# A sandwich of attention and feed-forward layers: the window mask moves from TensorE to VectorE's maximum, a state factor to ScalarE, and quantisation work to other turns

## Time and profile before

| | us |
|---|---|
| median of 3 runs (lowest to highest) | 1960.5 (1960.32 to 1961.45) |
| the profiled execution: its own time | 1959.31 |
| its span | 1957.5 |
| TensorE busy (matmuls) | 1876.3 |
| VectorE busy | 1433.4 |
| ScalarE busy | 1229.4 |
| GpSimd busy | 1235.9 |

### The profile page before, as it was taken

The page is one execution under the profiler, slowest core; times in us unless marked ns, Lnnn a source line. Parts: engine busy times, 40 slices in busy tenths (PEclk is TensorE's granted clock), DMA queues, the critical chain, the costliest instruction groups (busy, mean ns, idle before and its releaser), DMA issues.

```text
span 1957.5 us, 42161 instructions
## 1 busy us (share of the span) xinstructions
PE 1876.3 (96%) x11698; PEld 1252.8 (64%) x11698; DVE 1433.4 (73%) x3926; ACT 1229.4 (63%) x4840; POOL 1235.9 (63%) x1150
## 2 busy tenths in 40 slices
PE   4999999999999999999999999999989979999997
PEld 3667677777777777776777676777666635444443
DVE  6998888888888888888888888888899644302022
ACT  5777777777777777777777777776666535312121
POOL 3777777777777777777777777777677521212121
PEclk8999999999999999999999999999999989999999
DMA  5000000000000000000000000000100042000000
GB/s 199 25 26 25 26 25 24 24 24 24 32 25 24 24 24 24 29 24 24 24 24 24 30 29 24 24 24 13 54 13 7 7 134 79 26 1 22 0 21 21
DMA packets 44353, 61.43 MB, mean 31 GB/s; under 512 B 4928, under 2 KB 18496, under 8 KB 44288
## 3 DMA queue, kind: packets, MB, share of 16 engines
q1 hardware_dynamic: 44288, 60.64, 9.6%
HBM read 47.97 MB, written 12.65 MB: 31 GB/s over the span
## 4 chain that ended last, share of the span: by engine, by line
PE 62%; DVE 16%; issue 14%; POOL 3%; ACT 2%; DVEq 1%; DMA 0%; SPq 0%; POOLq 0%; ACTq 0%
PE bank L1250 18%; PE bank L1239 8%; PE bank L1278 6%; PE bank L1221 4%; PE bank L1294 4%; PE bank L1315 4%; PE bank L1379 3%; PE bank L1287 3%; DVE f_s L963 2%; PE bank L1205 2%; PE bank L1304 2%; POOL hl L527 2%; DVE f_nrm L953 2%; PE bank L1270 1%; PE bank L1297 1%
## 5 line engine op out<-in xcount | busy, mean ns | idle before, releaser
L488 POOL TENSOR_TENSOR f_acc<-f_acc,f_s 128x512 f32<-128x512 f32 (+1 forms) x416 | 534.3, 1284 | 30.6 <-POOL f_acc L488 0.4
L1250 PE MATMUL bank<-wh,xh 128*128 (+2 forms) x1024 | 334.9, 327 | 7.3 <-DVE cumh L1099 6.2
L1250 PE MATMUL bank<-wl,xh 128*128 (+2 forms) x1024 | 335.0, 327 | 0.0
L1250 PE MATMUL bank<-wh,xl 128*128 (+2 forms) x1024 | 334.7, 327 | 0.0
L469 POOL TENSOR_TENSOR pr<-pr,rp 128x512 f32<-128x512 f32 x128 | 133.0, 1039 | 229.5 <-DVE rp L894 229.5
L963 DVE TENSOR_SCALAR f_s<-f_nrm 128x512 f32<-128x512 f32 (+1 forms) x480 | 240.9, 561 | 3.7
L575 ACT ACTIVATE qe<-bank,nqm 128x128 f32<-128x128 f32 x512 | 180.8, 365 | 80.3 <-DVE qs L823 57.2
L527 POOL TENSOR_TENSOR hl<-hf,hh 128x512 f16<-128x512 f32 (+1 forms) x44 | 50.8, 1155 | 283.7 <-ACT hh L754 283.7
L1379 PE MATMUL bank<-xh,w 128*128 (+3 forms) x704 | 224.8, 382 | 3.8 <-ACT sg L748 3.8
L603 ACT ACTIVATE pr<-bank,pmx 128x128 f32<-128x128 f32 x512 | 180.9, 367 | 37.5 <-DVE pmx L887 29.6
L1239 PE MATMUL bank<-wh,oT 128*128 (+1 forms) x512 | 194.0, 379 | 3.8 <-DVE xl L1019 1.4
(11 more groups left out here) (177 smaller groups left out, 4973.7 us busy)
## 6 DMA issues: line engine op xcount, KB each, us to landing
f_raw<-wf SPq DMA_DIRECT2D x30, 256.0 KB, 2.6
dequantised<-f_dq SPq DMA_DIRECT2D x30, 256.0 KB, 2.0
wt<-dequantised SPq DMA_DIRECT2D x30, 256.0 KB, 3.0
raw_qkv<-wq SPq DMA_DIRECT2D x29, 256.0 KB, 2.5
raw_o<-wo SPq DMA_DIRECT2D x29, 256.0 KB, 2.6
rows<-x SPq DMA_DIRECT2D x4, 1024.0 KB, 9.3
xr<-x SPq DMA_DIRECT2D x16, 256.0 KB, 3.6
out<-yo SPq DMA_DIRECT2D x16, 256.0 KB, 2.1
```

Of the source, the lines that this page charges most:

```text
L488: nc.gpsimd.tensor_tensor(f_acc[:, 0:w], f_acc[:, 0:w], f_s[:, k % 8, 0:w], ALU.add)\
L1250: last = nc.tensor.matmul(dst, av, w[:, sl + c, lo:hi], start=(n == 0), stop=(n == 3 * NC - 1))
```

## The change

The mask is no longer added by a matmul. `p_max` first writes one element (`pause`) and then runs four `tensor_tensor_reduce`, one per head and 128 columns: each adds the mask to the scores, negates the sum, writes it back to SC, and gives its minimum to `pmx`. `p_exps` reads the negated scores with scale -1. For the first tile of a step, where the mask differs by sequence, ScalarE copies the first 128 columns of it to `win0` (`head_mask`), and TensorE's `scores` waits for that copy. `em` is made by ScalarE as an exponential with a bias of 0 or -1e30, right after the other decays, and VectorE's multiply and its wait go. `nf4_blocks` of piece i + 1 is made at p = 1 of step i, behind the compares (piece 0 still at p = 0), and the compares are spread 2, 3, 5, 5.

```diff
-NF4_STEPS = (range(0, 2), range(2, 6), range(6, 11), range(11, 15))
+NF4_STEPS = (range(0, 2), range(2, 5), range(5, 10), range(10, 15))
...
+            def head_mask(t):
+
+                if t.p == 0:
+                    nc.scalar.activation(win0[:], win[:, t.i % 2, 0:P], ACT.Copy).then_inc(s["head_mask"], 1)
+
...
                 nc.scalar.activation(edT[:, r, :], SM[:, P:P + 130], ACT.Exp)
+                if t.p == 0 and not (isinstance(t.i, int) and t.i == 0):
+                    nc.scalar.activation(em[:, 0, :], SM[:, 2 * P:2 * P + 1], ACT.Exp,
+                                         bias=keep[:].unsqueeze(2)[:, t.i % 2, :])
                 nc.scalar.activation(ked, ked, ACT.Exp, scale=-1.0).then_inc(s["dec_ev"], 1)
...
-                                                bias=pmx[:, r, j:j + 1],
+                                                bias=pmx[:, r, j:j + 1], scale=-1.0,
...
                 k_exps(t)
+                head_mask(t)
...
-                nc.vector.tensor_reduce(pmx[:, r, :], SC[:].rearrange("p (h n) -> p h n", h=GRP), AX.X, ALU.max,
-                                        negate=True).then_inc(s["pmx_d"], 1)
+                nc.vector.memset(pause[:], 0.0)
+                for j in range(GRP):
+                    sl = slice(j * P, (j + 1) * P)
+                    mask = win[:, 1, sl] if t.p or j >= 2 else win0[:]
+                    last = nc.vector.tensor_tensor_reduce(SC[:, sl], SC[:, sl], mask, -1.0, -MASKED, ALU.add,
+                                                          ALU.min, pmx[:, r, j:j + 1])
+                last.then_inc(s["pmx_d"], 1)
...
                 if nxt.p == 0:
-                    nc.vector.tensor_tensor(em[:, 0, :], scale, keep[:, nxt.i % 2:nxt.i % 2 + 1] if isinstance(nxt.i, int)
-                                            else keep[:].unsqueeze(2)[:, nxt.i % 2, :], ALU.mult).then_inc(s["em_d"], 1)
-                    dve.wait_ge(s["em_d"], nxt.i)
                     scale = em[:, 0, :]
...
-                if t.p == 0:
-                    nf4_blocks(t.i)
-                else:
+                if t.p:
                     nf4(t)
+                elif isinstance(t.i, int) and t.i == 0:
+                    nf4_blocks(0)
+                if t.p == 1 and not (isinstance(t.i, int) and t.i == STEPS - 1):
+                    nf4_blocks(t.i + 1)
...
-                nc.tensor.matmul(SC[:], identb[:], win[:, 1, :] if t.p else win[:, t.i % 2, :], start=True, stop=False)
+                if t.p == 0:
+                    pe.wait_ge(s["head_mask"], t.i + 1)
...
-                                                start=False, stop=(j == 3))
+                                                start=(j == 0), stop=(j == 3))
...
-    keep = np.ones((P, 2), np.float32)
-    keep[:, 0] = 0.0
+    keep = np.zeros((P, 2), np.float32)
+    keep[:, 0] = MASKED
```

More of the change, by code:

```diff
@@ L214, in layer @@
         rp = sb("rp", [P, 2, GRP])
+        pause = sb("pause", [P, 1])
+        win0 = sb("win0", [P, P], BF16)
         f_max = sb("f_max", [P, 2, NF4_MAX // BLK])
@@ L245, in layer @@
             kmx_d nkm_a kabs_ev kneg_d krope_d g_d gl_d rks_d kt_d qmx_d nqm_a qrope_d rq_d qt_d pmx_d
-            rp_d pm_d pa_ev su_d em_d sr_d acc_d qrope_p krope_p qn_p pn_p
+            rp_d pm_d pa_ev su_d head_mask sr_d acc_d qrope_p krope_p qn_p pn_p
             wqk_sc wqk_hi wqk_lo wo_sc wo_hi wo_lo w0_hi raw_a raw_b consts z_id
```

## The result

| | before | changed |
|---|---|---|
| median | 1960.32 us (1958.51 to 1961.45, 5 runs) | 1970.52 us (1969.92 to 1971.79, 5 runs) |
| ratio | | 1.0054, 95% interval 1.004 to 1.0069 |
| span of the profiled execution | 1957.5 us | 1969.8 us |

The change made the kernel 10 us slower, 0.5%, clear of the noise. I had forecast 1948 us with a range of 1925 to 1974: the time lies inside the range, but on the side to which I had given 0.24.

What follows compares the result with a forecast made beforehand. TensorE bounds, VectorE near. A middle group: 46.80 - 0.86 (mask) - 0.81 (old wait) + 0.65 (turn 3) + 0.50 (turn 0) = 46.28; 24 groups -12.5 us, others about 0: 1948.0 us, range 1925 to 1974.

Steps and rivals of the forecast that it cites:

- Step 1: Mask matmul leaves TensorE: where TensorE sets the pace, a turn falls from 11.50 to 11.28 us, 0.86 us a group.
- Step 2: The maxima cost more on VectorE: between +0.3 and +1.15 us a turn, taken as +0.65.
- D: What the maxima cost VectorE more than before, per turn; forecast +0.65 us.
- Rival (a): VectorE becomes the bound, nothing in the maxima overlapping (1.15 to 1.2 us a turn): 1984 us, weighed about 1972; chance 0.24.
- Step 3: Turn 3 gets a fifth compare and D: its VectorE stretch ends 1.05 us later, leaving 0.65 us of new wait.
- Step 4: Turn 0 loses 1.81 us of block maxima, D comes back, -1.16; stall between nothing and 0.8, taken as 0.5 us.
- the port: VectorE's waits for GpSimd, at f_nrm, compares, f_safe and em; in turn 0 to take at most 0.8 us.
- Rival (b): Turn 0's compares and f_nrm lose all the block maxima gave, 0.8 for 0.5: about 1961 us, no change; chance 0.10.
- Step 5: em and its wait, 0.90 us a group, leave VectorE behind the merge: priced at nothing to -0.1 us; ScalarE's extra nothing.
- Step 6: Turns 1 and 2 don't stall: turn 1 takes 1.3 us against about 1.5 of room, turn 2 takes D alone.
- The outer turns: The 31 turns outside the middle 96: about 0 in all, between -6 and +10 us.

Runs made afterwards that it cites:

- Run 1: The kernel before with only the mask moved into VectorE's maxima; compares 2-4-5-4, block maxima at p = 0, em on VectorE: 1970.8 us, ratio 1.0059.
- run 3: The changed kernel with the compares put back from 2-3-5-5 to 2-4-5-4: 1963.43 us, ratio to before 1.0024.
- run 10: The kernel before with em alone made by ScalarE: 1961.21 us, ratio to before 1.0007.
- run 8: The changed kernel with f_nrm ahead of the reciprocal that waits for ScalarE in turn 0, and compares 3-3-5-4: 1927.26 us, ratio to before 0.9834.
- run 9: As run 8, but with the mask back on TensorE and one reduction for the maxima: 1935.81 us, ratio to before 0.9878.
- runs 5 and 6: GpSimd's second to fourteenth adds of a piece cut to 8 of 512 columns, weights incomplete: changed kernel 1906.06 us, kernel before 1925.86 us.

## Why the prediction was wrong

- **Step 1** (11.28 us where TensorE sets the pace) was right, in turns 1 and 2.
- **Step 2** took D as 0.65; it is 0.36, near the lower end. The second small instruction is there, as I had reckoned, but overlaps: 0.25 us for the pair. Rival (a), slower because D is near 1.15, is refuted: the side was right, the mechanism was not.
- **Step 3** gave turn 3 a stall of 0.65; it was 0.49. Right in mechanism: compares contended, the fifth free. Run 1 shows that its sum came near by luck: D alone, with four compares, stalls 0.61 in turn 3. The spread also puts three adds instead of four into turn 2, which I hadn't priced, and that gave back more than the fifth compare cost: with four, run 3, turn 3 is 12.22 and not 11.77. Against that, the block maxima in turn 1 push GpSimd's adds back (runs 1 and 3), which I hadn't priced either.
- **Step 4** is the one that failed. I took 1.81 us of block maxima as won, gave D back, and put the stall of turn 0 at 0.5, at most 0.8. It is 1.53. One term was missing and one too small. The reciprocal behind the block maxima waits for ScalarE, and half of the freed time ended there (0.90 us); I looked at what the removed work delayed and not at what it covered. And I named the port but capped its cost at what the step had won. Each of the three port-sharing instructions there waited until a GpSimd instruction ended: they lost 1.17 us more than before. The fifth add that I had named makes 0.82 of that: with four (run 3) the same three instructions take 2.55 us against 3.37, and the stall is 0.71, although the wait for ScalarE stays. Rival (b) had that mechanism, with too small a price.
- **Step 5** was right (run 10). **Step 6** was right for the changed kernel as far as it went: turns 1 and 2 did not stall; what the block maxima do there to GpSimd's later adds it left out.
- **The outer turns** were put at 0, between -6 and +10: +4.8, inside, but not taken apart.

With turn 3 as measured and step 4 as I had it, the group would have been 46.12, a gain of 16 us; the 1.03 us missing in turn 0, times 24, is 25 us. Turn 3's smaller stall gave 4 us of that back, so the middle turns miss the forecast by 21 us (47.15 against 46.28 a group), and the outer turns by 5 more.

## What to carry to other kernels

Before work is moved out of a busy stretch, find the first instruction behind it that waits for another engine: of the time that is freed, only what exceeds that wait is won. Where the work goes to, look for what waits behind it on other engines too. Count VectorE's port-sharing instructions that fall while GpSimd runs back to back: here each waited for the end of a GpSimd instruction (a compare of 0.34 us took up to 1.5), so put them into gaps of VectorE, or behind GpSimd's last. And judge one edit with the order that suits it: the mask in the maxima cost about 11 us in the order of before (run 1) and gained 8.5 with f_nrm in the gap and compares 3-3-5-4 (run 8 against run 9).

## What the hardware showed

- The operation with a result beside its output is two instructions in VectorE's trace, of 0.33 and 0.14 us, and a pair starts 0.25 us after the last, 0.05 more than a plain operation of the size. The memset ahead of them costs nothing that shows: the first operation starts 1.10 us after the first scores matmul (841.64 against 840.54), the single reduction before started 1.09 after it.
- They did not wait for GpSimd: about 0.33 us each from 841.85 on, while adds ran. The Trainium skill, "SBUF — State Buffer", section "Who interferes with whom", says that a VectorE instruction with at most one SBUF input, outside the two-port modes, does not contend; this trace agrees.
- Eight columns of f_safe took 0.90 us on average before, among GpSimd's adds, and 0.17 in the changed kernel, where GpSimd has run out of adds at that point:

```profile
L944 DVE SCALAR_TENSOR_TENSOR f_safe<-f_max 128x8 f32 x24 | 21.6, 899 | 0.8
```

```profile
L957 DVE SCALAR_TENSOR_TENSOR f_safe<-f_max 128x8 f32 x24 | 4.0, 168 | 0.8
```

What stays open: how much of the loss is VectorE's wait at the port and how much GpSimd's own lateness, since runs 5 and 6 take away both; why the outer turns are 2.3 us longer with 4-4-4-3 than with 3-3-5-4 was not taken apart, and neither were the 4.8 us of the outer turns in the changed kernel.
